# Cross-attention and neighbour kernel: the output projection leaves VectorE for ScalarE and GpSimd, and SyncE's queue is put in another order

## The chip, the cores and the metric

The kernel runs on one core of one Trainium2 chip. The metric is the device time of one execution in microseconds. Engines are named TensorE (PE), VectorE (DVE), ScalarE (ACT), GpSimd (POOL) and SyncE (SP, which here only issues DMAs).

## What is computed

Four layers run over a batch of 32 sequences with 128 channels and 1024 positions. Layers 0, 1 and 3 are chunked cross-attention. Their queries, keys and values all come from `ctx` and not from the previous layer's output, so they don't wait for one another except through the residual. Layer 2 finds each position's 30 nearest neighbours in `ctx`, and adds a weighted sum of the neighbours' `x`.

```python
# one attention layer (0, 1, 3), chunks of 64 positions, 8 heads of 16
scores = einsum('bnqhd,bnkhd->bnhqk', qh, kh) * scale   # + NEG where masked
attn = softmax(scores)
out = einsum('bnhqk,bnkhd->bnqhd', attn, vh).reshape(N, T, C)
out = out @ W_out.T + b_out
out = out.transpose(0, 2, 1) * masks
out = out + x
out = (out - mean) * rsqrt(var + EPS)
# layer 2
idx = top_k(2 p.p' - |p|^2 - |p'|^2, 30)      # p = ctx[:, 0:3]
rel = pts[idx] - pts                          # spherical features of rel -> 3 batch norms -> att
out = x + einsum('bnkc,bnk->bnc', x[idx], softmax(att))
```

The line that the change touches is the projection `out @ W_out.T + b_out` with its multiplication by the mask.

## The kernel before

The program has three stages. The first (`attention_and_neighbours`) does the attention of all three layers and the neighbour search; it takes the first 4970 us or so. The second (`batch_norms`) and the third (`neighbour_sum`) follow it and are not touched.

**Steps.** The first stage is an order written out by hand. A batch (one sequence) has 24 steps: 3 layers of 8 steps, a step being 128 positions (two chunks) of one layer. A loop body holds 2 batches (48 steps) and runs 16 times (`all_steps`; the first and the last are unrolled, those between are a hardware loop). After the last comes a tail of 48 steps with what lags behind. Each engine has its own function `step(i, s)`, and each walks the same steps in the same order; semaphores hold them together. Step numbers below are those within a batch (0 to 23); work of the batch before is told as such.

What a step s does on each engine:

- TensorE computes the scores SC(s) (L584, L589), which need the block-diagonal keys `k_bd`; projections of q, k, v for the next layer (L537, L544); half a tile of distances PD (L602, L603) in two steps of three; the transpose of the probabilities of step s-3 (L610); the product with v of step s-4 (L618); every fourth step (0, 4, 8, ...) the output projection of four finished steps (L569); and the fetches G of neighbour coordinates (L559), which are matmuls with a one-hot matrix made from `low_all`. SC(s) stands first in the step, so TensorE is normally some microseconds ahead of the others.
- VectorE takes the row maxima of SC(s) (L1032, called row_max(s) below), the reciprocal of the row sums of step s-1 (L1040), then 3 or 4 operations of the top-32 search over 1024 distances (MAX8 L1017, FIND_INDEX8 L1024, MATCH_REPLACE8 L1019). In steps 1, 5, 9, 13, 17 and 21 (`r % 4 == 3`, with r = s - LAG_Y) it also evicts the output projection: one SCALAR_TENSOR_TENSOR (L1055) computes (PSUM + bias) * mask for 128x512 into `y_b`. In steps 14 and 22 it computes the statistics of the layer norm (L1066, L1067, L1070), which wait until GpSimd has added the residual. Every third step (L1091) it turns a 1 MB tile `low_all` of the previous batch's low index bytes into a one-hot matrix.
- ScalarE evicts projections, evicts PD into `dist` (L696), takes the exponentials of SC(s) (L703), evicts the transpose (L710) and the product with v (L716), applies the layer norm (L722), and evicts G (L729).
- GpSimd multiplies the probabilities of step s-1 by the reciprocals (L817), makes the distance row for the next batch (steps 17 to 22, L795 to L805), adds the residual `xb` to `y_b` (L831, for the first two layers of a batch: steps 9, 13, 17 and 21), computes the layer norm's scale, and does the selection (L895 to L898) and the geometry of the previous batch.
- SyncE issues all DMAs in program order and waits before many of them; whatever stands behind a waiting one waits too.

**SyncE's order.** In even steps it issues the keys of two later steps: `keys_of_heads` (L407 to L418) is eight small DMAs that put k_t on the diagonal of `k_bd`; those issued in step s are read by SC(s+4) and SC(s+5), so the keys issued in step 6 are for SC(10) and SC(11). The low index bytes of the previous batch go to a scratch in HBM in step 5 (L463, after `topped` and the `nbr` store L458), and come back broadcast over 128 partitions as `low_all`: tiles 0 and 1 in step 6 (`LOW_IN_AT`), tiles 2 to 7 in steps 12, 15, 18, 21, 24 and 27 (`SELECT_AT`), that is, the last two in steps 0 and 3 of the batch after. `load_low` (L500 to L506) first waits until TensorE has fetched from the tile that was in the buffer before:

```python
sp.wait_ge(fetched, at_least(i, START + 2 * (tile - 1), START))
alone(sp)
sp.dma_start(low_all[:, t % 2, :], dram["low"][i * BPB + v][t:t + 1].broadcast_to(...)).then_inc(low_in[t % 2], 16)
```

For tile 1, loaded in step 6, that is the previous occupant's last fetch, which TensorE makes in step 8. For the tile that is loaded in step 0 it is a fetch of step 23.

In `step` of SyncE the keys come first, then the columns, `ctx`, x2, the `nbr` store and the low bytes, y3, and the later low tiles last.

## Time and profile before

| what | value |
|---|---|
| three runs | 6666.72, 6674.75, 6677.72 us (median 6674.75) |
| the profiled execution, its own time | 6667.89 us |
| its span in the profile | 6665.9 us |
| VectorE busy over the span | 5886.1 us (88%) |
| TensorE busy | 5685.7 us (85%) |
| ScalarE busy | 4461.5 us (67%) |
| GpSimd busy | 3249.3 us (49%) |
| granted TensorE clock, mean | 0.904 |
| DMA, mean | 85 GB/s, 564.50 MB |

The span is the profiled execution from its first to its last record; 2 us lie around it. Busy shares are means over three stages with different limits, and the change touches only the first, so that stage has to be read alone. "Idle before" in a row is how long the engine had stood still when the instruction began, and the releaser is what it had waited for.

### The profile page before, as it was taken

The page shows a single profiled execution, that of the slowest core. Times are in us where ns is not written, and L with a number is a line of the kernel's source. Part 1 is how long each engine was busy: PE and PEld are TensorE (multiplying, and loading weights), DVE is VectorE, ACT ScalarE, POOL GpSimd, SP SyncE. Part 2 cuts the span into 40 slices and gives each one's busy share as a digit, 9 for nine tenths or more (in the row PEclk, how much of TensorE's full clock was granted, in tenths as well). Part 3 has the DMA queues.
Part 4 walks back from the last instruction along what each step waited for, and adds up shares of the span by engine and source line. Part 5 has one row for each costly group of instructions (what it writes and reads, how often), then busy time and mean ns, then how long its engine had stood idle before and what let it go on. Part 6 is the DMA issues. An engine that isn't in the chain of part 4 may idle for free. (4 is left out here: it accounts for less than half of the span.)

```text
span 6665.9 us, 228315 instructions
## 1 busy us (share of the span) xinstructions
PE 5685.7 (85%) x83284; PEld 3456.0 (52%) x83284; DVE 5886.1 (88%) x8332; ACT 4461.5 (67%) x17049; POOL 3249.3 (49%) x3279
## 2 busy tenths in 40 slices
PE   7888888888888888888888888888839949999998
PEld 3454545455555545545554555555423337677776
DVE  7999999999999999999999999999946588777776
ACT  7787878787787878787877878788822533333333
POOL 3455655555555555555655555555550023333332
PEclk9999988898888999898898998998859979999999
DMA  2333333233333333333233333333241013333332
GB/s 48 89 97 85 93 91 91 84 91 87 100 92 91 97 85 94 91 90 91 85 92 102 91 91 92 93 91 90 80 118 35 0 38 90 90 83 89 87 84 78
DMA packets 633780, 564.50 MB, mean 85 GB/s; under 512 B 535517, under 2 KB 557277, under 8 KB 598653
## 3 DMA queue, kind: packets, MB, share of 16 engines
q1 hardware_dynamic: 632572, 548.75, 29.1%
q8 instruction: 716, 11.73, 0.7%
q14 instruction: 492, 4.02, 0.2%
HBM read 380.55 MB, written 67.24 MB: 67 GB/s over the span
## 5 line engine op out<-in xcount | busy, mean ns | idle before, releaser
L703 ACT ACTIVATE prob<-SC,row_max 128x64 f32<-128x64 f32 x6144 | 1835.3, 327 | 671.7 <-DVE row_max L1032 664.8
L817 POOL TENSOR_TENSOR prob<-prob,row_rec 128x512 f32<-128x512 f32 x768 | 829.9, 1081 | 1897.7 <-DVE row_rec L1040 1897.1
L703 ACT ACTIVATION_READ_ACCUMULATOR prob<-SC,row_max 128x1 f32 x6144 | 1349.0, 220 | 0.0
L1024 DVE FIND_INDEX8 nbr<-top,dist 128x8 uint16<-128x1024 f32 x1024 | 1235.8, 1220 | 0.0
L1017 DVE MAX8 top<-dist 128x8 f32<-128x1024 f32 x1024 | 1194.1, 1207 | 12.6 <-DVE y_b L1055 10.3
L610 PE MATMUL PT<-ident,prob 128*128 128x128 f32 x3072 | 516.1, 295 | 573.9 <-ACT prob_t L710 563.2
L610 PEld LDWEIGHTS PT<-ident,prob 128*128 128x128 f32 x3072 | 383.6, 151 | 1076.8 <-issue 1033.2
L589 PE MATMUL SC<-k_bd,q_t 128*64 128x256 f32 x6144 | 935.8, 430 | 0.0
L1019 DVE MATCH_REPLACE8 dist<-top,dist 128x1024 f32<-128x1024 f32 x768 | 925.2, 1210 | 0.0
L1816 DVE TENSOR_TENSOR d_oh_a<-lo,iota_a 128x4096 bf16<-128x4096 bf16 x256 | 584.4, 2293 | 255.2 <-PE DM L1667 254.8
L1708 ACT ACTIVATE dense<-DM 128x512 f32<-128x512 f32 x512 | 305.6, 597 | 746.3 <-PE DM L1667 746.1
L559 PEld LDWEIGHTS G<-table,low_all 128*128 128x128 bf16 x24576 | 673.4, 97 | 196.8 <-issue 129.4
L559 PE MATMUL G<-table,low_all 128*128 128x24 bf16 x24576 | 708.3, 174 | 52.1 <-DVE low_all L1091 31.9
L1667 PEld LDWEIGHTS DM<-placed,d_oh_a 128*128 128x128 bf16 x24576 | 646.2, 96 | 113.5 <-issue 101.8
L1667 PE MATMUL DM<-placed,d_oh_a 128*128 128x32 bf16 x24576 | 651.8, 177 | 33.0 <-DVE d_oh_a L1816 28.4
L589 PEld LDWEIGHTS SC<-k_bd,q_t 128*64 128x64 f32 x6144 | 404.7, 147 | 331.0 <-issue 236.5
L1032 DVE TENSOR_REDUCE row_max<-SC 128x8 f32<-128x512 f32 x768 | 521.0, 678 | 43.8 <-PE SC L589 43.7
L603 PE MATMUL PD<-ctx 128*128 128x512 f32 x1024 | 546.2, 615 | 0.0
L710 ACT ACTIVATE prob_t<-PT 128x512 f32<-128x512 f32 x768 | 491.2, 640 | 2.2 <-PE PT L610 2.2
L537 PE MATMUL PJ<-ctx,w_in 128*128 128x512 f32 x768 | 484.2, 716 | 0.0
L696 ACT ACTIVATE dist<-PD,xcol 128x512 f32<-128x512 f32 x512 | 365.4, 714 | 165.1 <-PE PD L603 149.5
L1645 PE MATMUL AG<-dense,x_t 128*128 128x512 f32 x1024 | 473.6, 605 | 1.2 <-issue 1.2
(194 smaller groups left out, 9538.6 us busy)
## 6 DMA issues: line engine op xcount, KB each, us to landing
low_all<-low_scratch SPq DMA_DIRECT2D x256, 1024.0 KB, 4.9
k_bd<-k_t SPq DMA_DIRECT2D x3072, 16.0 KB, 1.9
placed<-compact SPq DMA_DIRECT2D x256, 192.0 KB, 3.7
ctx<-in_ctx SPq DMA_DIRECT2D x32, 512.0 KB, 4.0
mask<-in_mask SPq DMA_DIRECT2D x32, 512.0 KB, 7.8
xb<-in_x SPq DMA_DIRECT2D x32, 512.0 KB, 4.3
x_scratch<-xb SPq DMA_DIRECT2D x32, 512.0 KB, 4.7
y_scratch<-y_b SPq DMA_DIRECT2D x32, 512.0 KB, 6.6
```

What stands on the lines that cost most here:

```text
L559: last = pe.matmul(G[:, g * 24:(g + 1) * 24], hot[:, t % 2, col:col + 128], table[:, v % BPB, part, :], start=(part == 0), stop=(part == 2))
L589: last = pe.matmul(bank[64 * ch:64 * ch + 64, cols], q_t[:, w % 2, here], k_bd[:, s // 2 % KEY_BUFS, s % 2 * 2 + ch, cols], start=False, s ...
L603: pe.matmul(PD[:, :], ctx[:, u, t * 128:(t + 1) * 128], ctx[:, u, h * HALF:(h + 1) * HALF], start=False, stop=True).then_inc(pd_ready, 1)
L610: last = pe.transpose(PT[:, m * 128:(m + 1) * 128], prob[:, r % 4, m * 128:(m + 1) * 128], ident[:, :])
L703: last = act.activation(prob[:, s % 4, g * CHUNK:(g + 1) * CHUNK], SC[:, s % 2, g * CHUNK:(g + 1) * CHUNK], ACT.Exp, bias=row_max[:, s % 2 ...
L817: pool.tensor_tensor(pr, pr, row_rec[:, r % 2, :].unsqueeze(2).to_broadcast([128, 8, CHUNK]), ALU.mult).then_inc(normed, 1)
L1017: dve.max(best, row).then_inc(top_step, 1)
L1019: dve.match_replace(row, best, row, NEG_BIG).then_inc(top_step, 1)
L1024: last = dve.max_index(nbr[:, uu % BPB, t, k * 8:(k + 1) * 8], best, row)
L1032: dve.tensor_reduce(row_max[:, s % 2, :], SC[:, s % 2, :].rearrange("p (h k) -> p h k", h=8), AX.X, ALU.max, negate=True).then_inc(maxed, 1)
L1667: last = pe.matmul(DM[:, x % DM_BANKS, (g % 16) * 32:(g % 16 + 1) * 32].rearrange("p (q m) -> p q m", q=4), oh_a[:, t % 2, g, :], placed[: ...
L1816: dve.tensor_tensor(oh_a[:, t % 2, :, :].rearrange("p g (a two) -> p g a two", two=2), lo2[:, u, t, :, :].unsqueeze(2).to_broadcast(wide), ...
```

## The change

Three edits.

1. VectorE's SCALAR_TENSOR_TENSOR of `r % 4 == 3` is removed, with the wait for its own result behind the last of a batch (`copied`, then `masked`). ScalarE evicts the projection with the bias instead (one ACTIVATE of 128x512 before its `dist` eviction), into `y_b`.
2. GpSimd multiplies `y_b` by the mask in place (one TENSOR_TENSOR of 128x512), for all three layers, before the residual's addition. The addition now waits for the multiplication (`y_masked`).
3. SyncE's order within a step: the low bytes' store, the load of tiles 0 and 1, and the load of the later tiles now stand before the keys. The `nbr` store moves to one step later, and y3 waits for GpSimd's multiplication (`y_masked`) and for `mask_row_ready`.

```diff
@@ SyncE's step
+                v = lagging(i, s, LOW_OUT_AT)
+                if v is not None:
+                    b = i * BPB + v
+                    sp.wait_ge(low_ready, START + b + 1)
+                    alone(sp)
+                    rows = dram["low"][b].rearrange("t (g q k) -> q g t k", q=4, k=KP)
+                    for q in range(4):
+                        sp.dma_start(rows[q], low[32 * q:32 * q + 32, :, :]).then_inc(low_out, 16)
+                v = lagging(i, s, LOW_IN_AT)
+                if v is not None:
+                    sp.wait_ge(low_out, START + (i * BPB + v + 1) * 64)
+                    alone(sp)
+                    for t in range(2):
+                        load_low(i, v, t)
+                at = lagging_tile(i, s, SELECT_AT)
+                if at is not None and at[1] + 2 < NT:
+                    load_low(i, at[0], at[1] + 2)
                 if real(i, s, STEPS) and s % 2 == 0 and real(i, s // 2 + KEY_BUFS - 1, STEPS // 2):
                     keys_of_heads(i, s // 2 + KEY_BUFS - 1)
+                v = lagging(i, s, LOW_IN_AT + 1)
+                if v is not None:
+                    b = i * BPB + v
+                    sp.wait_ge(topped, START + (b + 1) * NT)
+                    alone(sp)
+                    sp.dma_start(dram["nbr"][b], nbr[:, v % BPB, :, :].rearrange("p t k -> p (t k)")).then_inc(nbr_out, 16)
...
-                v = lagging(i, s, LOW_OUT_AT)
+                v = lagging(i, s, 6)
                 if v is not None:
                     b = i * BPB + v
-                    sp.wait_ge(topped, START + (b + 1) * NT)
+                    sp.wait_ge(y_masked, START + (b + 1) * 2 * LAYERS)
                     alone(sp)
-                    sp.dma_start(dram["nbr"][b], nbr[:, v % BPB, :, :].rearrange("p t k -> p (t k)")).then_inc(nbr_out, 16)
...
-                    sp.wait_ge(masked, START + b + 1)
+                    sp.wait_ge(mask_row_ready, START + b + 1)
                     alone(sp)
                     sp.dma_start(dram["y3"][b], y_b[:, y_half(LAYERS * v + 2), :]).then_inc(y3_out, 16)
...
@@ ScalarE's step, after the q, k, v evictions and before dist
+                r = s - LAG_Y
+                if real(i, r, STEPS) and r % 4 == 3:
...
+                    act.activation(y_b[:, y_half(r // PAIRS), h * HALF:(h + 1) * HALF], bank, ACT.Identity, bias=b_out[:, jj:jj + 1]).then_inc(free, 1)
@@ GpSimd's step
+                    mine = y_b[:, y_half(r // PAIRS), half]
                     copied(pool, i, ("y", r // PAIRS, h))
+                    landed(pool, mask_in, i, uu)
+                    pool.tensor_tensor(mine, mine, mask[:, uu % BPB, half], ALU.mult).then_inc(y_masked, 1)
...
+                    pool.wait_ge(y_masked, START + (i * BPB + uu) * 2 * LAYERS + 2 * jj + h + 1)
                     pool.tensor_tensor(y_b[:, y_half(r // PAIRS), half], y_b[:, y_half(r // PAIRS), half], xb[:, uu % BPB, half], ALU.add).then_inc(added, 1)
@@ VectorE's step
-                    dve.scalar_tensor_tensor(y_b[:, y_half(r // PAIRS), half], PJ[:, use_parity(i, use), :], b_out[:, jj:jj + 1], mask[:, uu % BPB, half],
-                                             ALU.add, ALU.mult).then_inc(pj_free[use_parity(i, use)], 1)
-                    if jj == LAYERS - 1 and h == 1:
-                        copied(dve, i, ("y", r // PAIRS, 0))
-                        copied(dve, i, ("y", r // PAIRS, 1))
-                        dve.sem_inc(masked, 1)
```

What stands where on SyncE in steps 5 to 8 of a batch, first before (`low_scratch<-low` is the store of the low bytes, `low_all<-low_scratch` a load of a tile, `k_bd<-k_t` one set of keys; `fetched` counts TensorE's fetches):

```order
L463 DMA low_scratch<-low 32x8x32 [waits low_ready]
L463 DMA low_scratch<-low 32x8x32 x3
L417 DMA k_bd<-k_t 16x4x64 [waits pj_free1,scored]
L417 DMA k_bd<-k_t 16x4x64 x7
L506 DMA low_all<-low_scratch 128x4096 [waits low_out,fetched]
L506 DMA low_all<-low_scratch 128x4096 [waits fetched]
L475 DMA y_scratch<-y_b 128x1024 [waits masked]
L477 DMA mask<-in_mask 128x1024
```

and now:

```order
L437 DMA low_scratch<-low 32x8x32 [waits low_ready]
L437 DMA low_scratch<-low 32x8x32 x3
L511 DMA low_all<-low_scratch 128x4096 [waits low_out,fetched]
L511 DMA low_all<-low_scratch 128x4096 [waits fetched]
L417 DMA k_bd<-k_t 16x4x64 [waits pj_free1,scored]
L417 DMA k_bd<-k_t 16x4x64 x7
L483 DMA y_scratch<-y_b 128x1024 [waits y_masked,mask_row_ready]
L485 DMA mask<-in_mask 128x1024
```

The keys of step 6 have moved from ahead of both loads to behind them, and with that behind the second load's wait for `fetched`.

On GpSimd, from step 13 (the second half of a layer) to the layer norm's scale, stood, with `prob` the multiplication of the probabilities and `rstd` the scale:

```order
L831 TENSOR_TENSOR y_b<-y_b,xb 128x512 [waits x_in0,pj_free1]
L817 TENSOR_TENSOR prob<-prob,row_rec 128x512 [waits recip_ready]
L839 TENSOR_SCALAR rstd<-moments 128x1 [waits moments_ready,applied0]
L841 TENSOR_TENSOR rstd<-rstd,pow_half 128x1 [waits pool_ln]
L844 TENSOR_SCALAR rstd<-moments,rstd 128x1 [waits pool_ln]
```

and now:

```order
L847 TENSOR_TENSOR y_b<-y_b,mask 128x512 [waits mask_in0,pj_free1]
L854 TENSOR_TENSOR y_b<-y_b,xb 128x512 [waits y_masked,x_in0]
L835 TENSOR_TENSOR prob<-prob,row_rec 128x512 [waits recip_ready]
L862 TENSOR_SCALAR rstd<-moments 128x1 [waits moments_ready,applied0]
L864 TENSOR_TENSOR rstd<-rstd,pow_half 128x1 [waits pool_ln]
L867 TENSOR_SCALAR rstd<-moments,rstd 128x1 [waits pool_ln]
```

The multiplication by the mask stands ahead of the addition, which waits for it, and VectorE's statistics wait for the addition.

## Rows read from the trace of the kernel before

**Rows 1.** Busy time by stretch: the attention loop: PE, PEld, DVE, ACT, POOL busy, PEclk
```profile
150.00:4845.00 4695.00, 4033.78 (x54485) 2363.86 (x54484) 4477.99 (x6918) 3761.26 (x15709) 2666.44 (x2846) 0.90 0.32 91
```

**Rows 2.** VectorE groups: line engine op, forms, count | busy us, mean ns | idle before <-releaser
```profile
L1017 DVE MAX8 top<-dist 128x8 f32<-128x1024 f32 x1024 | 1194.1, 1207 | 12.6 <-DVE y_b L1055 10.3 <-issue 0.8 <-DVE dist L1019 0.2
L1055 DVE SCALAR_TENSOR_TENSOR y_b<-PJ,b_out,mask 128x512 f32<-128x512 f32 x192 | 134.3, 700 | 0.0
```

**Rows 3.** Waits of VectorE in the attention loop: waiter <- releaser: us, times, longest
```profile
DVE low_all L1091 <- DMA low_all<-low_scratch: 109.8, 28, 6.0
DVE stats L1066 <- POOL y_b L831: 45.8, 30, 1.5
```

**Rows 4.** Timeline of VectorE, steps 13 to 14 and 22: start, length, instruction, [idle before]
```profile
2042.71 0.71 DVE L1055 SCALAR_TENSOR_TENSOR y_b<-PJ,b_out,mask 128x512 f32<-128x512 f32 x1
2043.33 0.09 DVE L1024 MATCH_VALUE_LOAD nbr<-top,dist 128x8 f32 x1
2049.23 0.69 DVE L1066 BATCH_NORM_STATS2 stats<-y_b 128x6 f32<-128x512 f32 x1 [1.52 <-POOL y_b L831]
2102.60 0.63 DVE L1066 BATCH_NORM_STATS2 stats<-y_b 128x6 f32<-128x512 f32 x1
```

**Rows 5.** Timeline of GpSimd, steps 13 and 21
```profile
2047.93 1.26 POOL L831 TENSOR_TENSOR y_b<-y_b,xb 128x512 f32<-128x512 f32 x1
2100.36 1.27 POOL L831 TENSOR_TENSOR y_b<-y_b,xb 128x512 f32<-128x512 f32 x1 [0.23 <-POOL sq L803]
```

**Rows 6.** Timeline of ScalarE, step 13
```profile
2040.48 0.75 ACT L671 ACTIVATE k_t<-PJ,k_bias 128x512 f32<-128x512 f32 x1
2042.72 0.32 ACT L703 ACTIVATE prob<-SC,row_max 128x64 f32<-128x64 f32 x1 [0.92 <-DVE row_max L1032]
```

**Rows 7.** SyncE's queue around step 24, and VectorE's wait there
```profile
2117.18 0.97 SPq L498 DMA_DIRECT2D sph_scratch<-angle  x2
2128.79 0.35 SPq L506 DMA_DIRECT2D low_all<-low_scratch  x1
2136.57 1.29 DVE L1091 TENSOR_SCALAR low_all<-low_all,iota_p 128x4096 bf16<-128x4096 bf16 x1 [3.97 <-DMA low_all<-low_scratch]
```

**Rows 8.** SyncE's queue at steps 6 to 8, and what landing takes (page)
```profile
1998.73 5.30 SPq L417 DMA_DIRECT2D k_bd<-k_t  x8
2004.46 13.12 SPq L506 DMA_DIRECT2D low_all<-low_scratch  x2
k_bd<-k_t SPq DMA_DIRECT2D x3072, 16.0 KB, 1.9
```

**Rows 9.** TensorE at steps 8 to 11, VectorE at steps 10 and 11
```profile
2015.62 1.36 PE L559 MATMUL G<-table,low_all 128*128 128x24 bf16 x48
2020.23 0.40 PE L584 MATMUL SC<-mask_row,ones 3*64 3x512 bf16 x2
2025.81 0.40 PE L584 MATMUL SC<-mask_row,ones 3*64 3x512 bf16 x2
2024.83 0.67 DVE L1032 TENSOR_REDUCE row_max<-SC 128x8 f32<-128x512 f32 x1
2029.06 0.68 DVE L1032 TENSOR_REDUCE row_max<-SC 128x8 f32<-128x512 f32 x1
```

**Rows 10.** The same two places in a batch with TensorE at full clock
```profile
948.54 1.36 PE L559 MATMUL G<-table,low_all 128*128 128x24 bf16 x48
959.54 0.68 DVE L1032 TENSOR_REDUCE row_max<-SC 128x8 f32<-128x512 f32 x1
```

**Rows 11.** TensorE after two idle stretches; then stretches: lengths and granted clock (PEclk)
```profile
2087.15 1.09 PE L610 MATMUL PT<-ident,prob 128*128 128x128 f32 x4 [5.07 <-ACT prob_t L710]
2092.60 1.98 PE L589 MATMUL SC<-k_bd,q_t 128*64 128x256 f32 x8
2087.20:2096.10 8.90, 8.90 (x82) 4.63 (x83) 8.90 (x14) 7.59 (x26) 3.36 (x3) 0.51 0.13 30
2241.10:2246.00 4.90, 4.90 (x72) 3.15 (x72) 4.90 (x8) 3.64 (x20) 1.61 (x2) 0.50 0.08 13
```

More of the change, by code:

```diff
@@ L266, in attention_and_neighbours @@
         o_ready = sem("o_ready")
-        masked = sem("masked")
+        y_masked = sem("y_masked")
         added = sem("added")
@@ L477, in step @@
                         sp.dma_start(mask[:, v % BPB, :], dram["mask"][b + BPB].broadcast_to([128, T])).then_inc(mask_in[v % BPB], 16)
-                at = lagging_tile(i, s, SELECT_AT)
-                if at is not None and at[1] + 2 < NT:
-                    load_low(i, at[0], at[1] + 2)
                 v = lagging(i, s, OWN_AT)
@@ L689, in step @@
                         projection(i, name, rel, h)
+                r = s - LAG_Y
+                if real(i, r, STEPS) and r % 4 == 3:
+                    jj, uu = place(r)
+                    h = (r % PAIRS) // 4
+                    bank, free = produced(i, ("y", r // PAIRS, h))
+                    if h == 0:
+                        if jj == 0:
+                            act.wait_ge(applied[1], START + i * BPB + uu)
+                        elif jj == 1:
+                            act.wait_ge(y3_out, START + (i * BPB + uu) * 16)
+                        else:
+                            act.wait_ge(applied[0], START + i * BPB + uu + 1)
+                    act.activation(y_b[:, y_half(r // PAIRS), h * HALF:(h + 1) * HALF], bank, ACT.Identity, bias=b_out[:, jj:jj + 1]).then_inc(free, 1)
                 if real(i, s, STEPS) and s % SPAN < 2:
```

34 lines of the change are left out of this document (4 added, 30 removed).

## The prediction

> **What bounds the kernel now.** I read the busy time by stretch first, because the page's shares are means over three stages. In the attention loop VectorE is busy 4478 of 4695 us, 95%, against 4034 for TensorE, 3761 for ScalarE and 2666 for GpSimd [rows 1]. So VectorE bounds the stage, and the stage is worth what VectorE's work and idle time in it are worth. The groups of VectorE come next: the eviction that is to leave has 192 instances of 700 ns, with no idle time before them, and the MAX8 behind some of them waited 10.3 us in all for the eviction's own result [rows 2]. Then VectorE's waits in the loop: 109.8 us in 28 instances for the DMA of a `low_all` tile, and 45.8 us in 30 for GpSimd's residual addition, never over 1.5 us [rows 3]. These two waits and the eviction are what the three edits touch.
>
> **Edit 1 and 2, what VectorE loses.** The eviction starts at 2042.71 and the next instruction at 2043.33, so one is worth 0.62 us and not its 0.71 [rows 4]. 192 of them are 119 us, and the drain behind them 10 us.
>
> ScalarE gets 192 evictions of the kind of the `k_t` one, 0.75 us. In step 13 it then idles 0.92 us for the row maxima [rows 6]. In steps where it idles less, a start of the exponentials that is up to 0.75 us later costs nothing, since VectorE needs them only one step later, and a step of VectorE is 4.2 us at the least (2024.83 to 2029.06, [rows 9]). I cost this at nothing; the cover is that step. If it were gone, the 192 would cost up to 0.75 us each, 144 us.
>
> **Edit 2, what GpSimd gains.** A multiplication of 128x512 in place is an operation like the residual's, and a following one that depends on it starts 0.23 us after its end [rows 5]: with 1.24 us from start to start I take 1.47 us for it. Most of GpSimd's time this is free. It is not free where VectorE waits for the addition. In step 13 the addition ends at 2049.19, and VectorE starts the statistics at 2049.23 after 1.52 us of idle time [rows 4, 5]. VectorE now comes 0.62 us earlier and GpSimd 1.47 us later, so that this wait grows by 2.1 us. It occurs in 30 batches [rows 3]: 63 us. At the second place, step 22, the addition ends at 2101.63 and the statistics start at 2102.60, a slack of 0.97 us; 1.47 + 0.62 - 0.97 gives a new wait of 1.1 us, 32 times: 36 us. Together 99 us, below which I see no way, since both ends of the chain are in the rows. If a wait of VectorE for TensorE stood right behind, it would hide some, so 80 to 110.
>
> GpSimd's slower operation speaks against the edit in another way too. The Trainium skill (GPSIMD Engine Reference, section 4.1, Engine selection) wants elementwise work on VectorE, because GpSimd needs about twice the time for two inputs. The trace agrees, 1.24 us against 0.62 us; by that rule alone the edit would lose 1.24 us of a free engine for 0.62 us of the bound one, and the rule doesn't say which counts.
>
> **Edit 3, the tile that came late.** The 28 waits for `low_all` are one per batch, at the tile loaded in step 0. Its load was issued at 2128.79, after the keys, `ctx` and x2; the geometry's stores ahead of them ended at 2118.15; VectorE waited until 2136.57, 3.97 us [rows 7]. Now the load stands right behind those stores. Between the two lie 10.6 us, or 9 if the geometry comes 1.5 us later through GpSimd's multiplication; the longest wait is 6.0 us [rows 3]. In half of the batches a hardware loop's seam may take some of that, so 100 to 110; I take the whole 109.8 us.
>
> **Edit 3, the keys that come late.** This is the term that decides. In step 6 the second `low_all` load waits for TensorE's fetch of step 8. SyncE had issued the keys for SC(10) and SC(11) at 1998.73, in 5.30 us, before it; the second load was out at 2017.58 (2004.46 + 13.12) [rows 8]. Now these keys come behind it. TensorE's fetch ended at 2016.98, and it started SC(10) at 2020.23 [rows 9]. The new order gives: keys from 2017.8, the eighth issued at about 2022.9, landed 1.9 us later [rows 8] at 2024.8, that is 7.8 us after the fetch. SC(10) thus starts 4.6 us late.
>
> TensorE is then idle for 4.6 us, and what its clock does afterwards decides the rest. Behind an idle stretch of 5.07 us it ran at the lower level, 1.2 GHz, for 8.9 us (granted clock 0.51), and an SC matmul group took 1.98 us; behind another stretch of the kind the lower level lasted 4.9 us (0.50) [rows 11]. With the small matmuls for the mask ahead I take SC(10) as 2.5 us there and 1.4 us at full clock, so it ends 10.3 us after the fetch. VectorE wanted it 7.85 us after the fetch in this batch (2024.83) and 9.64 us after it in a batch in which TensorE was at full clock before [rows 9, 10], both less 0.62 us for the eviction of step 9. The waits are 3.1 and 1.3 us. As VectorE's step 5 gets an eviction shorter, TensorE idles less before the fetch and more batches are of the second kind: 1.7 us. Then SC(11). From SC(10) to SC(11) TensorE needs 5.6 us at full clock [rows 9], and 2.5 to 3.9 us more at the lower level; VectorE needs 4.2 us. SC(11) ends 17.3 to 18.7 us after the fetch (7.8 + 5.6 + 2.5 or 3.9 + 1.4), VectorE is ready at 14.6: 2.7 to 4.1 us, I take 3.1. That makes 4.8 us in each of the 30 batches with a fetch ahead: 144 us. The bounds: 1.5 us a batch (45 us) if the clock stays up, 7.2 us (216 us) if every batch is like this one with the long lower stretch. After SC(11) VectorE's step of over 7 us lets TensorE get ahead again.
>
> The Trainium skill (TensorE: Matmul & The Clock Gate, section Why this matters for your kernels) warns of idle gaps between bursts of matmuls, which bring the clock down. With that rule the term is the 144 us, without it the 45 us. The rows above show the fall, so the sum has it.
>
> The other moves cost nothing: the later loads (steps 12, 18) now stand ahead of keys that are wanted four steps of at least 4.2 us later, and wait for a fetch of the step before only; y3 and `nbr` are wanted much later.
>
> **The sum.** -119 - 10 - 110 + 99 + 144 = +4 us on the profiled execution's 6667.9: **6672 us**. The median of the runs lies 7 us above that execution. So the forecast is that one order's gain and the eviction's gain are given back at two new waits.
>
> **Rivals.**
>
> - *The keys are late but cheap (faster).* TensorE keeps the upper level, or the keys are issued faster, so a batch loses 1.5 us: 4 - 99 = -95, 6573 us. If half of the stretches are cheap, some 6620. For it: the full-clock batches leave 1.8 us more room [rows 10]. Against it: rows 11.
> - *The keys are not late at all (faster).* Were the wait in step 6 to end by itself sooner, since all else moves up: -140, 6528 us. Against it: the wait is for a fetch that TensorE makes two steps later in any case.
> - *The keys are late and dear (slower).* The place is SC(10) and SC(11), the price 7.2 us a batch: 216 instead of 144, +76 us, 6744 us. It decides from 4.7 us a batch on, where the sum changes sign. For it: this batch by its own rows. Against it: half the batches have the room of rows 10.
> - *GpSimd blocks VectorE (slower).* The mechanism here would be that the 192 new operations hold VectorE's two-input or one-hot operations back, up to 1.24 us each for those they meet. VectorE spends 256 times 1.29 us [rows 7] in the one-hot ones, 330 us or 7% of the loop, so some 7% of the 241 us of new GpSimd time meets them, 17 us, 24 with the other two-input ones; 6696 us. The Trainium skill (SBUF — State Buffer, section Who interferes with whom) describes such an exclusive lock on a pair of ports.
>
> **How the numbers follow.** Forecast (6640 to 6705): 0.38. Cheap keys: 0.29, none late: 0.05, dear keys: 0.23, blocking: 0.05. About 0.2%, 13 us, is what a measurement of this kernel can tell from no change. Of the forecast's 0.38, 0.11 lies on the faster side of that, 0.16 within, 0.11 on the slower side; so faster 0.45, same 0.17, slower 0.38. The range takes the cheap and dear ends and leaves the rest out: 6575 to 6750.
>
> **What would show it.** Right: no L1055 on VectorE; waits for `low_all` in the loop near nothing; the statistics' wait at 3.6 us in step 14 and 1.1 us in step 22, about 140 us in all; row maxima waiting for SC at steps 10 and 11, about 1.7 and 3.1 us; SyncE waiting as long for G as before, now ahead of keys; granted clock about 0.5 around step 10. Wrong: VectorE's waits for SC under 60 us (cheap) or over 230 us (dear), waits for `low_all` that remain, or a wait of VectorE for the exponentials, which would say that ScalarE has become the bound.

## The result, and the profile after

The changed kernel takes **6704.43 us** (median of nine runs; eight lie between 6694.67 and 6721.17, a ninth was disturbed and is left out of the comparison). The kernel before takes 6673.73 us in nine runs. The ratio is 1.0049, with a 95% interval of 1.0038 to 1.006: the change makes the kernel **slower by 0.5%**, about 31 us. The forecast was 6672 us, no change. The time lies inside the forecast's range, but above its centre by 32 us, more than the 13 us that a measurement can tell. The profiled execution of the change took 6703.10 us, 35 us more than that of before.

I read the attention loop alone again. Its last row maximum starts at 4881 us now and started at 4838 us before, so the loop is 43 us longer; what follows it is 7 us shorter. Two windows that end there hold the same work, before first and then after. The columns are those of [rows 1]: length, then busy time of PE, PEld, DVE, ACT and POOL, then clock, DMA share and GB/s.

```profile
150.00:4838.00 4688.00, 4028.77 (x54399) 2360.25 (x54397) 4470.99 (x6906) 3755.78 (x15687) 2662.52 (x2842) 0.90 0.32 91
```

```profile
150.00:4881.00 4731.00, 4047.99 (x54372) 2383.20 (x54370) 4371.53 (x6721) 3856.67 (x15871) 2905.77 (x3027) 0.89 0.31 90
```

VectorE's busy time fell by 99 us, so the eviction did leave VectorE. But the loop grew by 43 us, so VectorE now stands idle 142 us longer. All of VectorE's waits in the loop (of 0.15 us or more) say where (waiter, releaser: us, times, longest):

```profile
DVE row_max L1055 <- PE SC L594: 196.2, 101, 4.0
DVE stats L1069 <- POOL y_b L854: 136.1, 60, 3.6
DVE moments L1073 <- DVE stats L1070: 9.1, 60, 0.2
DVE low L1128 <- DVE nbr_t L1126: 6.3, 28, 0.2
```

The waits for `low_all`, 109.8 us in [rows 3], are gone, and so is the drain of 10.3 us behind the eviction [rows 2]. The statistics' wait rose from 45.8 us [rows 3] to 136.1. The row maxima's wait for TensorE's scores rose from 23.5 us before to 196.2. The account of the loop closes: -99 - 110 - 10 + 90 + 173 = +44 us, where 43 were measured.

**The statistics.** Here is step 14, VectorE first and then GpSimd, from the page's timeline view (start, length, instruction, idle before):

```profile
2063.62 0.69 DVE L1069 BATCH_NORM_STATS2 stats<-y_b 128x6 f32<-128x512 f32 x1 [3.54 <-POOL y_b L854]
```

```profile
2055.29 0.73 POOL L937 TENSOR_TENSOR r<-sqr 128x256 f32<-128x256 f32 x1
2056.10 0.73 POOL L939 TENSOR_TENSOR r<-r,sqr 128x256 f32<-128x256 f32 x1
2057.02 1.50 POOL L942 TENSOR_SCALAR r2m<-r 128x512 f32<-128x512 f32 x1 [0.20 <-POOL r L939]
2058.50 1.50 POOL L943 TENSOR_SCALAR good<-r 128x512 f32<-128x512 f32 x1
2059.96 1.04 POOL L835 TENSOR_TENSOR prob<-prob,row_rec 128x512 f32<-128x512 f32 x1
2060.96 1.27 POOL L847 TENSOR_TENSOR y_b<-y_b,mask 128x512 f32<-128x512 f32 x1
2062.31 1.27 POOL L854 TENSOR_TENSOR y_b<-y_b,xb 128x512 f32<-128x512 f32 x1
```

ScalarE had its eviction long ready:

```profile
2054.09 0.75 ACT L707 ACTIVATE y_b<-PJ,b_out 128x512 f32<-128x512 f32 x1
```

The new multiplication starts at 2060.96, 6.1 us after ScalarE's eviction ended. In between GpSimd is never idle for more than 0.20 us: behind the end of its selection it does four operations of the previous batch's geometry (4.7 us) and the probabilities first. The wait is thus made of a backlog with the multiplication on top of it; experiments e7 and e8 take the two apart.

**The keys.** SyncE's queue in steps 6 to 8, then TensorE and VectorE at steps 9 to 11, of the changed kernel:

```profile
2013.56 13.04 SPq L511 DMA_DIRECT2D low_all<-low_scratch  x2
2026.86 5.13 SPq L417 DMA_DIRECT2D k_bd<-k_t  x8
```

```profile
2024.64 1.36 PE L564 MATMUL G<-table,low_all 128*128 128x24 bf16 x48
...
2033.40 0.40 PE L589 MATMUL SC<-mask_row,ones 3*64 3x512 bf16 x2 [4.08 <-DMA k_bd<-k_t]
2033.74 1.86 PE L594 MATMUL SC<-k_bd,q_t 128*64 128x256 f32 x8
2035.53 2.00 PE L542 MATMUL PJ<-ctx,w_in 128*128 128x512 f32 x2
...
2040.96 1.08 PE L594 MATMUL SC<-k_bd,q_t 128*64 128x256 f32 x8
```

```profile
2035.64 0.69 DVE L1055 TENSOR_REDUCE row_max<-SC 128x8 f32<-128x512 f32 x1 [2.52 <-PE SC L594]
2042.09 0.69 DVE L1055 TENSOR_REDUCE row_max<-SC 128x8 f32<-128x512 f32 x1 [2.12 <-PE SC L594]
```

The fetch ends at 2026.00. The loads' wait ends with it, and the keys are issued from 2026.86 on for 5.13 us. SC(10) starts at 2033.40, 7.4 us after the fetch and after 4.08 us of idle TensorE. Its main part then takes 1.86 us and not 1.08, and the projection 2.00 and not 1.12: the clock has fallen. VectorE waits 2.52 us at step 10 and 2.12 us at step 11. Summed by step over the trace, the row maxima wait 77.7 us at step 10, 77.9 at step 11 (30 times each), 26.8 at step 0 (16.5 before) and 11.7 at step 17 (1.9 before).

### The profile page after: what moved, and what is told of

Same layout as the page of the kernel before. It is cut to its first block and busy times, and to the rows that moved or that the text cites. A ratio compares the mean times of both kernels' runs of the same rounds, so it can differ in the third digit from the quotient of the medians.

```text
span 6701.2 us, 228797 instructions
## 1 busy us (share of the span) xinstructions
PE 5702.0 (85%) x83284; PEld 3480.0 (52%) x83284; DVE 5778.6 (86%) x8140; ACT 4567.1 (68%) x17241; POOL 3501.4 (52%) x3471
## 3 DMA queue, kind: packets, MB, share of 16 engines
q1 hardware_dynamic: 632572, 548.75, 29.1%
## 5 line engine op out<-in xcount | busy, mean ns | idle before, releaser
L835 POOL TENSOR_TENSOR prob<-prob,row_rec 128x512 f32<-128x512 f32 x768 | 801.7, 1044 | 1674.4 <-DVE row_rec L1063 1670.6
L721 ACT ACTIVATION_READ_ACCUMULATOR prob<-SC,row_max 128x1 f32 x6144 | 1365.8, 223 | 0.0
L589 PE MATMUL SC<-mask_row,ones 3*64 3x512 bf16 x1536 | 330.9, 425 | 242.1 <-DMA k_bd<-k_t 135.4
```

The costliest lines, as they stand in the source:

```text
L721: last = act.activation(prob[:, s % 4, g * CHUNK:(g + 1) * CHUNK], SC[:, s % 2, g * CHUNK:(g + 1) * CHUNK], ACT.Exp, bias=row_max[:, s % 2 ...
L835: pool.tensor_tensor(pr, pr, row_rec[:, r % 2, :].unsqueeze(2).to_broadcast([128, 8, CHUNK]), ALU.mult).then_inc(normed, 1)
```

## The experiments

Twelve kernels ran, each in three rounds beside the kernel before. That kernel's median was 6675.33, 6676.20 and 6675.06 us in the three groups, so one number, 6675, stands for it below. All ratios are to before.

| | SyncE's old order | the change's order (keys of step 6 late) | later tiles first, keys in time |
|---|---|---|---|
| VectorE evicts | 6675 (before) | 6718 (e2) | 6563 (e6) |
| ScalarE evicts, GpSimd multiplies | 6709 (e1) | 6704 (the change) | 6557 (e3) |

### e1: edits 1 and 2 alone

```diff
@@ SyncE's step of the changed kernel: the order of before
-                (low bytes' store, tiles 0 and 1, later tiles)
                 keys_of_heads(i, s // 2 + KEY_BUFS - 1)
+                (nbr store, low bytes' store, tiles 0 and 1)
                 y3
+                (later tiles)
```

> Edits 1 and 2 of the change with SyncE's old order (keys first, low bytes' tiles last). Theory (the change is the sum of independent terms): the eviction's 107 us of VectorE and the 10 us drain go, the statistics' wait for GpSimd grows by 90 us to about 136, the waits for low_all stay near 110, VectorE's waits for SC stay near 25 to 40. Sum -27: about 6647 us, faster than before by 0.4%. Rival (GpSimd's and ScalarE's added work itself costs, through contention or late exponentials): 6674 or more, VectorE's busy time in the loop falls by less than 90 us or a wait for the exponentials appears.

Measured: 6708.9 us, ratio 1.005 [1.0033, 1.0066], 62 us above the theory. VectorE's waits in its loop, without two that did not change:

```profile
DVE low_all L1094 <- DMA low_all<-low_scratch: 148.7, 29, 7.2
DVE stats L1069 <- POOL y_b L854: 131.8, 60, 3.6
DVE row_max L1055 <- PE SC L594: 48.0, 40, 3.5
DVE row_rec L1063 <- ACT prob L721: 2.9, 6, 0.6
```

The theory of independent terms falls. VectorE's busy time fell by 102 us (to 4369 us in the loop), and the statistics' wait grew as forecast. But the wait for `low_all` grew from 109.8 to 148.7 us, and that for the scores from 23.5 to 48.0. The rival named the right size for the wrong reason, since the wait for the exponentials is 2.9 us. So moving the eviction, taken alone, *costs* 34 us. VectorE coming earlier to things that are late anyway could only give its gain back. A loss needs something that is itself later, and for the tile of step 0 the trace shows it: counted from VectorE's row maximum of step 20, on the mean of 28 batches, the tile lands after 47.3 us in e1 and after 45.8 us before, while VectorE is ready for it after 42.2 and 42.1 us. e12 looks into where that comes from.

### e2: the queue's new order alone

```diff
@@ the kernel before, SyncE's step
+                (low bytes' store, tiles 0 and 1, later tiles)
                 keys_of_heads(i, s // 2 + KEY_BUFS - 1)
+                (nbr store, one step later)
-                (nbr store, low bytes' store, tiles 0 and 1)
                 y3 (now also waits for mask_row_ready)
-                (later tiles)
```

> SyncE's new order alone, the eviction with its mask still one operation of VectorE. Theory (sum of terms): waits for low_all vanish (-110), VectorE waits for SC at steps 10 and 11 about 2 to 2.6 us each (+120 to +156): 6685 to 6720 us, slower than before. With e1 near 6647 the two parts then add up to the change's 6704. Rival (the late keys cost only because VectorE became faster through edit 1, and hide beside its eviction otherwise): the waits at steps 10 and 11 stay under 1.5 us each (90 us), and the kernel is faster than before, under 6655.

Measured: 6718.01 us, ratio 1.0064 [1.0047, 1.0081]. The waits for `low_all` are gone, and the row maxima wait 74.1 us at step 10 and 80.8 us at step 11. They sum to 155 us, and in the change to 156: the late keys cost the same whether or not VectorE evicts, and edit 3 as it was made is a loss by itself. Its two halves are +155 and -110.

e1's +34 and e2's +43 add up to +77, and the change has +31. The two parts are not independent. The 39 us that e1 adds to the wait for `low_all` cannot occur when that wait is gone.

### e3: keys ahead of the first two tiles

```diff
@@ SyncE's step of the changed kernel
-                v = lagging(i, s, LOW_IN_AT)
-                if v is not None:
-                    ...
-                        load_low(i, v, t)
                 at = lagging_tile(i, s, SELECT_AT)
                 if at is not None and at[1] + 2 < NT:
                     load_low(i, at[0], at[1] + 2)
                 ...
                     keys_of_heads(i, s // 2 + KEY_BUFS - 1)
+                v = lagging(i, s, LOW_IN_AT)
+                if v is not None:
+                    ...
+                        load_low(i, v, t)
```

> The changed kernel with one line group moved: keys stand ahead of the load of tiles 0 and 1 (step 6), the later tiles' loads stay ahead of the keys. Theory (keys of step 6 held up behind the load's wait for the fetch cost 156 us): SC waits at steps 10 and 11 fall under 0.3 us each, low_all waits stay at nothing, 6704 - 156 = 6548 us, down to 6530 if the waits at steps 0 and 17 go with them. Rival (other late keys or the loads ahead of keys in steps 12, 15, 18 cost as well, or TensorE limits these steps anyway): 6600 or more with SC waits elsewhere. Rival 2: the statistics' wait, 136 us now, shrinks or grows by over 20 us, since VectorE arrives at another time.

Measured: 6557.49 us, ratio 0.9822 [0.9805, 0.9838], 147 us less than the change. In the loop:

```profile
DVE stats L1069 <- POOL y_b L854: 135.8, 60, 3.6
DVE row_max L1055 <- PE SC L594: 50.9, 41, 3.3
```

At steps 10 and 11 0.4 us of waiting is left, and none for `low_all`. The late keys are shown to be the cause of the 156 us. Of these 12 come back at step 0, where the wait rose from 26.8 us. The scores' wait of 50.9 us that remains (38.3 at step 0, 9.4 at step 17, 3 elsewhere) is the part that I had hoped might go, and it did not.

### e4 and e5: how much of the keys' price is the clock

```diff
@@ TensorE's step of the changed kernel, ahead of the wait for keys_in
+                    if s % BSTEPS == 10:
+                        for n in range(8):
+                            e = n % 2
+                            pe.matmul(bank[64 * e:64 * e + 64, 0:256], w_out[:, 0, 0:64], w_in[:, 0, 0:256], start=True, stop=True, skip_group_check=True)
```

e5 has `range(18)`. The scores that follow overwrite what these matmuls write.

> The changed kernel with eight extra matmuls (64 columns of weights by 256, float32, results overwritten) on TensorE in step 10 ahead of its wait for the keys, so that TensorE is busy for some 3 us of the 4.4 us in which it stood idle. Theory (a part of the cost is the clock that falls behind the idle stretch): granted clock around steps 10 and 11 near 1.0, VectorE's wait at step 10 falls from 2.6 to about 1.5 us and at step 11 from 2.6 to under 1: 6704 - 30*(1.1+1.6) = 6623 us. Rival (the keys' lateness alone sets both waits, the clock nothing): 6704 within 10 us. Rival 2 (the extra matmuls are themselves in the way): slower than 6704.

Measured: 6705.51 us, ratio 1.0044 [1.0027, 1.0061], the time of the change. By that number alone the clock would play no part. TensorE's timeline of e4 shows that the experiment did only in part what it was made for. Two batches, the same place in each:

```profile
2016.53 1.95 PE L588 MATMUL SC<-w_in,w_out 128*64 128x256 f32 x16
2021.21 0.63 PE L593 MATMUL SC<-mask_row,ones 3*64 3x512 bf16 x2 [2.73 <-DMA k_bd<-k_t]
2021.77 1.98 PE L598 MATMUL SC<-k_bd,q_t 128*64 128x256 f32 x8
...
2324.16 1.95 PE L588 MATMUL SC<-w_in,w_out 128*64 128x256 f32 x16
2329.22 0.40 PE L593 MATMUL SC<-mask_row,ones 3*64 3x512 bf16 x2 [3.11 <-DMA k_bd<-k_t]
2329.55 1.08 PE L598 MATMUL SC<-k_bd,q_t 128*64 128x256 f32 x8
```

In the first batch the eight matmuls took 1.95 us, TensorE stood idle for another 2.73, and SC(10) ran at the lower level all the same. In the second it stood idle for 3.11 us and SC(10) took 1.08 us, as at the upper level. Of the 30 batches with late keys SC(10) takes 1.08 us in 12, 1.2 to 1.95 in 11 and 1.98 in 7; in the change it takes 1.64 us or more in all 30. The waits at steps 10 and 11 are 125 us in e4, 30 less than in the change.

> As e4, with 18 extra matmuls instead of 8. In e4 the eight took only 1.95 us (16 records) and TensorE stood idle for another 2.5 us, and its clock fell as before; 18 take about 4.4 us and fill the idle stretch. Theory (clock): TensorE stays at the upper level, SC(10) takes 1.1 and not 2.0 us. The keys' lateness alone leaves VectorE about 2.0 us at step 10 (SC(10) starts 7.5 to 8.3 us after SC(9), takes 1.4, VectorE arrives at 7.2) and 1.4 us at step 11 (5.6 us of TensorE against 4.24 of VectorE), 3.4 us a batch where the changed kernel has 5.2: the attention loop 54 us shorter than in the changed kernel. Whole time 6650 us if the later stages are as in the changed kernel; e4's third stage was 32 us longer than the changed kernel's, and if that comes again, 6682. Rival (clock plays no part): loop within 10 us of e4's, SC waits 4.2 us a batch or more.

Measured: 6691.25 us, ratio 1.0021 [1.0011, 1.0032]. The same place in e5, and two stretches of 3.8 us from SC(10) on, first of the change and then of e5 (the clock is the third number from the end):

```profile
2006.44 4.11 PE L588 MATMUL SC<-w_in,w_out 128*64 128x256 f32 x36
2010.49 0.40 PE L593 MATMUL SC<-mask_row,ones 3*64 3x512 bf16 x2
2010.82 1.08 PE L598 MATMUL SC<-k_bd,q_t 128*64 128x256 f32 x8
```

```profile
2033.50:2037.30 3.80, 3.80 (x12) 1.35 (x12) 1.66 (x4) 0.00 (x0) 2.93 (x5) 0.55 0.95 272
```

```profile
2010.50:2014.30 3.80, 3.80 (x21) 1.84 (x19) 2.35 (x6) 0.92 (x2) 3.56 (x6) 1.00 0.95 287
```

Now the granted clock is 1.00 where it was 0.55, that is 2.4 GHz where it was mostly 1.2. SC(10) takes 1.08 us in all 30 batches. From SC(10) to SC(11) TensorE takes 5.58 us on the mean of the 30, and 7.88 in the change. The waits at steps 10 and 11 are 56.6 and 36.9 us, 62 less than in the change, and the loop is 51 us shorter (54 expected): the wait at step 0 grew by 13.5. So of the 156 us that the late keys cost, 62 are the clock's and 94 the lateness itself.

The rest of e5's program gave 36 us back, though nothing there was changed. From the last row maximum of the stage to the end of the span it is 1820.5 us in the change, 1856.0 in e4 and 1856.5 in e5. In the other kernels here it is 1822 to 1830. The last section comes back to this. A total that does not move can thus hide two effects of opposite sign: e4's loop is in truth 33 us shorter, as its waits at steps 10 and 11 say.

### e6: what the eviction's move is worth when the keys are in time

```diff
@@ the kernel before, SyncE's step
+                at = lagging_tile(i, s, SELECT_AT)
+                if at is not None and at[1] + 2 < NT:
+                    load_low(i, at[0], at[1] + 2)
                 ...
                     keys_of_heads(i, s // 2 + KEY_BUFS - 1)
...
-                at = lagging_tile(i, s, SELECT_AT)
-                if at is not None and at[1] + 2 < NT:
-                    load_low(i, at[0], at[1] + 2)
```

> The kernel before with one group moved: the loads of the later low_all tiles stand ahead of the keys; the store, the load of tiles 0 and 1 and VectorE's eviction stay as before. It is e3 without edits 1 and 2. Theory A (moving the eviction off VectorE is worth next to nothing while the statistics wait for GpSimd and TensorE's scores at steps 0 and 17 come late): waits for low_all gone, 6675 - 110 = 6565 us, within 15 us of e3's 6557. Theory B (the eviction's 117 us are a gain once SyncE's order is right, and e1 hid them by its longer low_all wait alone): 6557 + 27 = 6585 or more. Rival (the later loads ahead of keys hold other keys up): SC waits above 60 us, over 6600.

Measured: 6563.14 us, ratio 0.983 [0.9814, 0.9847]. Theory A holds: e3's 6557 is 6 us better, which the two intervals don't tell apart. In e6 the statistics wait 45.8 us and the scores 29.9; in e3 it is 135.8 and 50.9. What edits 1 and 2 take off VectorE (103 us of busy time, 4364 in the loop against 4467, and the 10 us drain) is given back by 90 and 21 us of waits. e3 also has the change's places for the store of the low bytes and for `nbr`, on which no wait of VectorE was seen. This is also the largest gain from one move on the kernel before among those tried: three lines, 112 us.

### e7: without the multiplication

```diff
-                    pool.tensor_tensor(mine, mine, mask[:, uu % BPB, half], ALU.mult).then_inc(y_masked, 1)
+                    alone(pool)
+                    pool.sem_inc(y_masked, 1)
```

The edit is made to e3.

> e3 without GpSimd's multiplication by the mask (left out of the computation; GpSimd only passes the semaphore on). Theory (the multiplication itself, 1.27 us in front of the addition, is what VectorE waits for): statistics' wait at step 14 falls from 3.54 to about 2.2 us, at step 22 from 0.98 to 0, the two-input operation of VectorE in step 18 goes back from 1.48 to 1.18 us: 6557 - 40 - 29 - 9 = 6480 us. Rival (GpSimd has slack elsewhere, the time is set by another chain): over 6530. In either case a wait of 2.2 us stays at step 14 that the multiplication does not explain: GpSimd is then in geometry operations of 4.7 us that stand ahead of the addition.

Measured: 6489.36 us, ratio 0.9719 [0.9703, 0.9735], 68 us less than e3. The statistics wait 65.6 us at step 14 (2.19 each) and not at all at step 22. Of 135.8 us 70 are gone. The multiplication itself explains that much of the wait, and as forecast 2.2 us stay at step 14 that it does not explain.

### e8: the geometry behind the addition

```diff
@@ GpSimd's features, in e3
-                v = lagging(i, s, R2_AT)
+                v = lagging(i, s, R2_AT + 1)
```

> e3 with GpSimd's four geometry operations of step 12 (r, r, r2m, good: 4.7 us) placed one step later, behind the multiplication and addition of step 13; nothing is left out. ScalarE has evicted y_b 6 us before GpSimd gets to it in e3. Theory (the statistics' wait at step 14 is GpSimd's backlog of geometry, not the speed of one multiplication): the wait falls from 3.54 us to under 0.5, the wait at step 22 stays 1.0: 6557 - 100 = 6457 us. Rival (the root on ScalarE, which now waits for good 3 to 4 us longer, delays the exponentials): a new wait of VectorE for the reciprocals or for SC at steps 15 to 17 gives back more than 40 us, over 6500.

Measured: 6434.74 us, ratio 0.9642 [0.9626, 0.9658]: 123 us less than e3, and 55 less than e7, with the multiplication in place. GpSimd and then VectorE at step 13 to 14:

```profile
1947.08 1.04 POOL L835 TENSOR_TENSOR prob<-prob,row_rec 128x512 f32<-128x512 f32 x1 [0.57 <-DVE row_rec L1063]
1948.08 1.28 POOL L847 TENSOR_TENSOR y_b<-y_b,mask 128x512 f32<-128x512 f32 x1
1949.43 1.28 POOL L854 TENSOR_TENSOR y_b<-y_b,xb 128x512 f32<-128x512 f32 x1
1950.67 0.73 POOL L937 TENSOR_TENSOR r<-sqr 128x256 f32<-128x256 f32 x1
```

```profile
1951.15 0.66 DVE L1069 BATCH_NORM_STATS2 stats<-y_b 128x6 f32<-128x512 f32 x1
```

The addition ends at 1950.71, and VectorE comes to the statistics at 1951.15 without a wait. The whole 3.54 us at step 14, of which before had 1.5, go when four operations in GpSimd's queue stand elsewhere. The theory holds, and the gain is 22 us more than forecast. The loop is 127 us shorter than e3's: 106 at step 14, 6 at step 22 (now 23.2 us), 10 of scores (40.9 us and not 50.9) and 10 of VectorE's busy time, less 5 us of new waits for the exponentials.

### e9 to e12: the same parts in other company

e9 is e6 with the edit of e8. e10 is the changed kernel with the edit of e8. e11 is e8 with one more move on GpSimd:

```diff
-                part = s % BSTEPS - SPLIT_AT
-                if real(i, s, STEPS) and 0 <= part <= SPLITS and real(i, u + 1, BPB):
-                    split_row(i, u + 1, part, START + i * STEPS + r + 1)
                 ...
                     pool.tensor_tensor(y_b[...], y_b[...], xb[...], ALU.add).then_inc(added, 1)
+                    if s % BSTEPS >= SPLIT_AT:
+                        pool.wait_ge(added, START + (i * BPB + uu) * 4 + 2 * jj + h + 1)
+                part = s % BSTEPS - SPLIT_AT
+                if real(i, s, STEPS) and 0 <= part <= SPLITS and real(i, u + 1, BPB):
+                    split_row(i, u + 1, part, START + i * STEPS + s - LAG_SUM + 1)
```

e12 is e1 with the edit of e7.

> e6 (VectorE evicts as before, later tiles ahead of the keys) with GpSimd's geometry of step 12 behind the addition of step 13, as in e8. It is e8 without edits 1 and 2. Theory (the eviction's move has its own worth of 117 us on VectorE, but in the change the statistics' wait took most of it back): the statistics' wait of 46 us goes, 6563 - 46 = 6517 us, so that e8's 6435 makes the move worth 82 us (117 less the 23 us wait at step 22, less some scores that come late). Rival (VectorE is no longer the bound here, the move is worth little in either order): within 25 us of e8, under 6460.

Measured: 6513.53 us, ratio 0.9756 [0.974, 0.9772]; 6517 was expected. The eviction's move is worth 79 us here, against e8, and 6 us between e6 and e3. The difference is whether GpSimd's addition is in time.

> The changed kernel, keys late as in it, with GpSimd's geometry of step 12 behind the addition of step 13 and nothing else. Theory (the statistics' term and the keys' term are independent): 106 us of wait at step 14 go, the waits at steps 10 and 11 stay at 156 us in all: 6704 - 110 = 6594 us. Rival (VectorE, sooner at each step, meets later scores at steps 16, 17 and 0, so that part is given back): over 6620.

Measured: 6589.48 us, ratio 0.9873 [0.9857, 0.989]; 6594 was expected. The statistics' term is independent of the keys' term: 115 us here, 123 with the keys in time.

> e8 with the multiplication and addition of y_b ahead of the part of the distance row in the same step of GpSimd (2.1 us of subtraction in step 21), with one more wait of GpSimd for its own addition. Theory: VectorE's wait for the statistics at step 22, 23 us in all, goes: 6435 - 20 = 6415 us. Rival (the distance row or the geometry, now later, is late for others, or VectorE is only late elsewhere): 6430 or more.

Measured: 6419.27 us, ratio 0.9613 [0.9597, 0.9629]; 6415 was expected. VectorE no longer waits for the statistics at step 22. But of these 23 us 16 come back as waits for scores (57.4 us and not 40.9), and the loop is only 7 us shorter than e8's: the rival, that VectorE is only late elsewhere, came true in part. This is the fastest kernel of the study, 256 us (3.9%) under the kernel before and 285 under the change, though its step over e8 alone is no wider than the intervals.

> e1 (ScalarE evicts, SyncE's old order) without GpSimd's multiplication by the mask, which is left out of the computation. Question: why e1's wait for low_all is 149 us and not before's 110. Theory (half of the 39 us is VectorE, which comes 0.65 us earlier in step 1; the other half is SyncE's store of the angles, 0.7 us later in step 23 since GpSimd's multiplications delay the geometry, with keys and the tile's load behind it): the wait falls to 120 to 132 us, the statistics' wait to 66 and nearly 0; 6709 - 40 - 26 - 9 - 20 = 6614 us. Rival (the wait grows by as much as VectorE gains anywhere, since the load's time is fixed by another chain): the wait grows to 170 or more, and the time stays above 6640.

Measured: 6616.73 us, ratio 0.9913 [0.9897, 0.993]; 6614 was expected. So e1's +34 us has two parts: the eviction moved to ScalarE without GpSimd's multiplication is worth -58 us, and the multiplication costs 92. Its waits:

```profile
DVE low_all L1095 <- DMA low_all<-low_scratch: 122.0, 29, 5.9
DVE stats L1070 <- POOL y_b L855: 65.5, 30, 2.2
```

The wait for `low_all` is 122 us: of e1's 39 extra us 27 go with GpSimd's multiplication, and 12 stay. The path that would carry it is SyncE's store of the angles, which waits for GpSimd's geometry, with the keys and the tile's load behind it in the queue. The traces fit. Counted from the row maximum of step 20 as above, this store is issued after 28.9 us before, 30.0 in e1 and 29.1 in e12, and the tile lands after 45.8, 47.3 and 46.2. VectorE is ready for it after 42.1 to 42.2 us in all three, so the half of the 39 us that the expectation put down to an earlier VectorE was not there, and the right total is in part luck. That the 27 us hang on the multiplication is shown; that they pass through this store was not tried by itself.

## Why the prediction was wrong

Two effects that the sum put at nothing were not nothing: later scores, +17 us, and contention, +16 us. By the prediction's own steps:

- **What bounds the kernel, what VectorE loses.** Right. The eviction's 0.62 us times the 186 that lie in the window are 115 us. Busy time fell by 99, and the 16 us between are contention (below). The 10 us drain and the 110 us of `low_all` went as forecast.
- **What GpSimd gains, +99.** Right within 10%: 3.55 us at step 14 and 0.99 us at step 22 on the mean of 30, where 3.6 and 1.1 were forecast, +90 us in all. I read the end of the addition and took the 1.5 us that before had as given. What GpSimd did ahead of it was not looked at, and e8 shows that this was the larger part. That did not spoil the number, but it hid the best move. The rule of the Trainium skill (GPSIMD Engine Reference, section 4.1), that elementwise work belongs on VectorE since GpSimd needs about twice the time for two inputs, would make edits 1 and 2 a loss. By itself e1 agrees (+34 us) and e9 against e8 does not (-79 us): what decides is whether somebody waits for GpSimd there.
- **The keys, +144.** The mechanism was right: the queue's wait ends with the fetch, the keys follow, TensorE's clock falls, VectorE waits twice. The size came out at 155.6 us (2.59 and 2.60 us a batch). The first wait was forecast at 1.7, because half of the batches should have had the room of [rows 10]. They did not. In 23 of the 30 batches VectorE's row maxima of step 9 start within 2 us of TensorE's SC(9), as in the batch shown, and there the first wait is 2.3 to 4.0 us. The second wait was forecast at 3.1 and is 2.60, as the lower clock lasted less long (7.88 us from SC(10) to SC(11), not 8.1 to 9.5). The two errors partly cancel; +12 us remain. Behind the total the split was off as well, so its nearness is partly luck: the forecast gave 45 us to the lateness and 99 to the clock, and e5 gives 94 and 62.
- **"The other moves cost nothing", and ScalarE at nothing.** This is the step that failed first: ScalarE's added evictions were costed at nothing under the cover of one step of VectorE. The row maxima also wait longer for the scores of steps 0 and 17 and a little less at step 1, +17 us. e3 against e6 has it too, 50.9 against 29.9 us, without a late key. So it belongs to edits 1 and 2, not to the order. e7 has 63 us of such waits without the multiplication, so that is not its cause. Nor is it only that VectorE comes earlier to scores as late as ever: the scores themselves are later. From step 12 to step 17 VectorE takes the same time in e6 and e7 (29.6 and 29.7 us from row maximum 12 until it is ready for row maximum 17, mean of 29 batches), but SC(17) ends 0.85 us later in e7, and TensorE waits 0.93 us longer there for the probabilities that ScalarE evicts. That is close to the 0.75 us of ScalarE's new eviction, which stands ahead of them in its order. It points to ScalarE; no run takes that eviction away by itself, so the cause is argued and not shown. The waits at step 0 also sit at the hardware loop's seam: they fall in 13 batches only, each the first of a pass through the loop body, and in each TensorE stands idle for 3.4 us or more ahead of SC(0) for nothing that the profile shows, in the kernel before as in the change.
- **Contention.** That GpSimd's new operations hold VectorE back was a rival, at +24 us, of which 17 in the one-hot operations. It came true beside everything else: the one-hot operations take 11 us more in the loop and the two-input maximum of step 18 takes 5 us more (last section), 16 in all. It should have stood in the sum and not among the rivals. Its size was estimated from GpSimd's added time, which e7, e8 and e12 don't bear out (last section).

Against the forecast's +4 us this gives: keys +12, scores of other steps +17, contention +16, statistics -9, and +4 for the six evictions of the first batch, which end before the window and brought nothing there; +44, as the loop shows. The later stages' -7 make it 37, and the profiled execution shows 35. The sum was five terms of about 100 us with opposite signs, so errors of 10 to 17 us in some of them were enough to move the result out of "no change"; a sum of this kind deserves less weight on its centre. The dear-keys rival was too dear (216 us, and 156 were measured). The forecast's 6672 us also stand on the profiled execution, which lay 7 us under the median; the same sum on the median gives 6679.

The sum also took each part as worth the same in any company. e1 shows that it isn't: by the sum's own terms edits 1 and 2 alone would have gained 30 us (-119 - 10 + 99), and they cost 34. Without GpSimd's multiplication they gain 58 (e12), so the multiplication costs 92 there, near the forecast's 99, but through a later tile as well as through the statistics.

## What to carry to other kernels

When work is taken off the engine that bounds a stage, list what that engine waits for next, and look at what the late producer was doing just before: here moving four operations of GpSimd's queue gained 123 us (e8), and leaving out the operation added gained 68 (e7). A wait in an in-order DMA queue delays everything behind it, so ask of each reordering which issue now stands behind a wait for something that happens two steps later, and move only the issues that don't. Compare by stage, since e4's total hid a loop that was 33 us shorter.

## What the runs showed of the hardware

**Unchanged code became slower.** In e4 and e5 the third stage is about 36 us longer than in the change, though only the first stage of TensorE's program had matmuls added. TensorE's group there, in the 1779 us behind the end of the loop, first the change and then e5 (busy, mean ns, idle before with releasers):

```profile
L1670 PE MATMUL DM<-placed,d_oh_a 128*128 128x32 bf16 x24000 | 636.5, 177 | 32.3 <-DVE d_oh_a L1819 28.6 <-DMA placed<-compact 1.0 <-issue 0.2
```

```profile
L1674 PE MATMUL DM<-placed,d_oh_a 128*128 128x32 bf16 x23232 | 621.5, 177 | 66.6 <-issue 34.7 <-DVE d_oh_a L1823 24.6 <-DMA placed<-compact 4.7
```

34.7 us of idle time have appeared in which TensorE waits for nothing that the profile shows, and the granted clock from 700 us after the loop on is 0.94 and not 0.96:

```profile
5580.00:6680.00 1100.00, 1026.49 (x23523) 782.45 (x23520) 851.38 (x750) 346.24 (x552) 386.55 (x257) 0.96 0.32 87
```

```profile
5530.00:6680.00 1150.00, 1053.28 (x23703) 795.38 (x23699) 853.76 (x753) 349.65 (x557) 386.08 (x257) 0.94 0.31 84
```

It repeats in e4, with 26.5 us of such idle time. The Trainium skill (Runtime: NRT & Kernel Launch, section Instruction fetch mechanics) says that a taken branch to a page of code that is not at hand stalls the engine, and so the place of the code could matter; no run here tests that, and the cause stays open.

**VectorE beside a busier GpSimd.** The one-hot operation of the low bytes, 245 times in the loop, before and after:

```profile
L1091 DVE TENSOR_SCALAR low_all<-low_all,iota_p 128x4096 bf16<-128x4096 bf16 x245 | 313.9, 1281 | 109.8 <-DMA low_all<-low_scratch 109.8
```

```profile
L1094 DVE TENSOR_SCALAR low_all<-low_all,iota_p 128x4096 bf16<-128x4096 bf16 x245 | 325.2, 1327 | 0.0
```

Its mean rises from 1281 to 1327 ns. It is 1340 in e3, still 1315 in e7 and 1327 in e12 without the multiplication, and 1285 in e8 with it: what counts is which operation of GpSimd it meets, more than how many there are. In the change the 184 one-hot operations with no operation of GpSimd beside them take 1268 ns on the mean, and the 30 that meet GpSimd's multiplication or addition of `y_b` take 1741, up to 2335; in e8 the 30 that meet them take 1371. The maximum of step 18 (min/median/max of 32), before and after:

```profile
L1096 DVE TENSOR_TENSOR sqr<-r2m,r x32: 693/1182/1192, 405.0 to 4951.2; 128x512 f32<-128x512 f32 x32
```

```profile
L1099 DVE TENSOR_TENSOR sqr<-r2m,r x32: 693/1322/1484, 405.9 to 4991.2; 128x512 f32<-128x512 f32 x32
```

In e7 its mean in the loop is back from e3's 1316 to 1175 ns, where before has 1167; in e8, with the multiplication and the other order, it is 1445. The Trainium skill (SBUF — State Buffer, section Who interferes with whom) says that VectorE in its two-port modes, and with two SBUF inputs against GpSimd's reads, shares ports with GpSimd, and that the one that comes second waits. The trace agrees in direction: the one of these maxima with no operation of GpSimd beside it is the fastest, 693 ns, and the median is 489 ns more already before the change.

**The clock.** In e4 an idle stretch of 2.73 us behind 1.95 us of added matmuls was followed by the lower level in one batch, and one of 3.11 us was not in another. Of the 30 idle stretches at that place, 1.8 to 3.3 us long, 12 left SC(10) at 1.08 us. The length of the idle stretch alone does not decide it. In the change, with 3.6 to 5.3 us, none did; in e5, with at most 1.03 us, all did.
